# Four graph layers on one core: other distances, within 128 bytes, between the weights and what they are multiplied with

## What is computed

```
layer 0: q, k, v = x@Wq.T+bq, x@Wk.T+bk, x@Wv.T+bv     # 8 heads of 32
         P = softmax(where(adj == 0, -16384, q@k.T));  z = v
         4 times: z = 0.9 * P@z + 0.1 * v;              x = LN(x + z)
layer 1: P = softmax(where(adj == 0, -inf, (x@Wq)@(x@Wk).T / 16))   # one head
         x = LN(x + P@(x@Wv)@Wo + bo)
layer 2: 8 heads, P = softmax(where(adj == 0, -inf, q@k.T / sqrt(32)))
         x = LN(x + (P@v)@Wo + bo)
layer 3: for labels d = 1..4: agg_d = (adj == d) @ x / count_d
         out = relu(concat(agg_d)@Wd.T + bd)
         r, z = sigmoid(out@Wri.T + x@Wrh.T + b), sigmoid(out@Wzi.T + x@Wzh.T + b)
         n = tanh(out@Wni.T + bni + r*(x@Wnh.T + bnh)); x = LN((1-z)*n + z*x)
```

## The kernel before

| tensors | before |
|---|---|
| w_hi, w_lo, ident, wT (masks) | 0 |
| layer 0's q, k, z, v, E, PT | 32 |
| layer 1's q, v, E, PT, xT1 | 96 |
| layer 2's q, k, v, E, PT, and zT2 in the place of q and k | 64 |
| xw (also oT), agg, xT3, gates rT, zT, nT | 64 |
| y0 to y3, xn0, xn1 | 32 |
| xT_hi0 to 3, xT_lo0 to 3 | 64 |

## Time and profile before

### The profile page before, as it was taken

The page is one execution under the profiler, slowest core; times in us unless marked ns, Lnnn a source line. Parts: engine busy times, 40 slices in busy tenths (PEclk is TensorE's granted clock), DMA queues, the critical chain, the costliest instruction groups (busy, mean ns, idle before and its releaser), DMA issues.

```text
span 1605.4 us, 44598 instructions
## 1 busy us (share of the span) xinstructions
PE 1547.1 (96%) x17360; PEld 1405.8 (88%) x17360; DVE 1282.8 (80%) x3164; ACT 1237.9 (77%) x4074; POOL 697.0 (43%) x710
## 2 busy tenths in 40 slices
PE   7888999999999999999999999999999999999986
PEld 6777999899899989998998999899899999998875
DVE  3676888888888888888888888888888888888764
ACT  4677887787888788888878788887878888787652
POOL 1344444434454444445444444544444444444411
PEclk7999999999999999999999999999999999999999
DMA  5100000111110011011001101100110110000000
GB/s 201 34 25 28 28 28 15 34 35 29 34 35 28 15 35 34 28 35 35 27 15 35 35 28 35 34 28 15 35 35 28 35 35 27 15 28 25 18 8 13
DMA packets 71425, 51.64 MB, mean 32 GB/s; under 512 B 4400, under 2 KB 69936, under 8 KB 70576
## 3 DMA queue, kind: packets, MB, share of 16 engines
q1 hardware_dynamic: 71216, 48.79, 10.0%
HBM read 40.39 MB, written 8.39 MB: 30 GB/s over the span
## 4 chain that ended last, share of the span: by engine, by line
PE 67%; ACT 28%; DVE 2%; issue 1%; DMA 1%; POOL 0%; SPq 0%; POOLq 0%; DVEq 0%; ACTq 0%
ACT E L706 9%; PE bank_A L400 7%; ACT E L770 7%; PE bank_B L400 7%; PE bank_B L629 6%; PE bank_A L444 6%; PE bank_C L400 5%; PE bank_B L444 4%; PE bank_A L629 3%; PE bank_A L418 3%; PE bank_B L412 3%; ACT PT L712 2%; PE bank_A L430 2%; PE bank_X L550 2%; PE bank_A L528 2%; PE bank_B L438 2%
## 5 line engine op out<-in xcount | busy, mean ns | idle before, releaser
L850 POOL TENSOR_TENSOR E<-E,rsum 128x512 f32<-128x512 f32 x256 | 270.7, 1058 | 472.5 <-DVE rsum L1041 317.6
L858 POOL TENSOR_TENSOR rstd<-var,minus_half 128x2 f32<-128x2 f32 x128 | 93.7, 741 | 407.9 <-DVE var L995 407.9
L712 ACT ACTIVATE PT<-bank_C 128x512 f32<-128x512 f32 x128 | 85.8, 670 | 59.9 <-PE bank_C L438 59.9
L1002 DVE TENSOR_SCALAR y<-y,mv,rstd 128x256 f32<-128x256 f32 x192 | 93.0, 527 | 25.8 <-POOL rstd L858 25.8
L943 DVE COPY_PREDICATED_SCALAR bank_A<-absent,fill 128x512 f32 x128 | 92.3, 742 | 15.2 <-PE bank_B L430 14.4
L400 PE MATMUL bank_A<-xT_hi,w_hi 128*128 128x256 f32 x384 | 99.7, 284 | 0.0
L400 PE MATMUL bank_A<-xT_hi,w_lo 128*128 128x256 f32 x384 | 97.1, 277 | 0.0
L943 DVE COPY_PREDICATED_SCALAR bank_B<-absent,fill 128x512 f32 x128 | 94.7, 740 | 0.0
L770 ACT ACTIVATE E<-bank_A,nmax 128x128 f32<-128x128 f32 x256 | 92.4, 402 | 2.5 <-DVE nmax L1037 2.5
L706 ACT ACTIVATE E<-bank_B,nmax 128x128 f32<-128x128 f32 x256 | 94.2, 435 | 0.0
L706 ACT ACTIVATE E<-bank_A,nmax 128x128 f32<-128x128 f32 x256 | 90.8, 382 | 4.1 <-DVE nmax L946 4.1
(11 more groups left out here) (225 smaller groups left out, 6299.3 us busy)
## 6 DMA issues: line engine op xcount, KB each, us to landing
xt_in<-in_xt SPq DMA_DIRECT2D x64, 128.0 KB, 2.3
absent<-in_adj SPq DMA_DIRECT2D x64, 128.0 KB, 2.7
x_in<-in_x SPq DMA_DIRECT2D x32, 256.0 KB, 3.0
out<-y SPq DMA_DIRECT2D x32, 256.0 KB, 2.2
adj<-in_adj SPq DMA_DIRECT2D x32, 128.0 KB, 3.3
adjT<-in_adjt SPq DMA_DIRECT2D x32, 128.0 KB, 3.1
stage<-in_weights SPq DMA_DIRECT2D x3, 1024.0 KB, 11.3
row<-in_rows SPq DMA_DIRECT2D x1, 1024.0 KB, 7.9
```

The lines of the kernel that those rows point to most:

```text
L712: nc.scalar.activation(PT0[:, part].rearrange("p g c n -> p (g c n)"), C0[:, :], ACT.Copy, scale=1.0 - ALPHA).then_inc(pt0_ready.sem, 1)
L850: nc.gpsimd.tensor_tensor(e, e, rs[:, part].unsqueeze(2).to_broadcast([P, SB, P]), ALU.mult).then_inc(e_sig.sem, 1)
L858: nc.gpsimd.tensor_tensor(rstd[part][:], var[part][:], minus_half[:], ALU.pow)\
L1002: a = nc.vector.tensor_scalar(y[part][:, g, :], src[g], mv[part][:, g, 0:1], rstd[part][:, g:g + 1], ALU.subtract, ALU.mult)
```

## The change

One gap grows, one goes, and four small ones come in between the split inputs, which are now placed layer by layer (hi and lo of a layer side by side) and not all hi and then all lo. No instruction, wait, transfer, size or order differs on any engine; only addresses do.

```
-        sb("gap_1", [P, 16])
+        sb("gap_1", [P, 24])
         xw = sb("xw", [P, 8 * D])
         agg = sb("agg", [P, G, D])
...
         xn = [sb(f"xn{L}", [P, G, D]) for L in range(2)]
-        sb("gap_2", [P, 40])
-        xT_hi = [sb(f"xT_hi{L}", [P, NC, GN], F32R) for L in range(4)]
-        xT_lo = [sb(f"xT_lo{L}", [P, NC, GN], F32R) for L in range(4)]
+        xT_hi, xT_lo = [], []
+        for L, gap in enumerate((24, 16, 24, 8)):
+            sb(f"gap_x{L}", [P, gap])
+            xT_hi.append(sb(f"xT_hi{L}", [P, NC, GN], F32R))
+            xT_lo.append(sb(f"xT_lo{L}", [P, NC, GN], F32R))
         stats = [sb(f"stats{L}", [P, G, 6]) for L in range(4)]
```

## The result

The changed kernel takes 1622.2 us (median of 4 runs, 1620.83 to 1625.17), the kernel before beside it 1608.57 us (4 runs, 1606.68 to 1610.14): a ratio of 1.0087, 95% interval 1.0069 to 1.0104. It is slower, by 13.6 us. The forecast was 1602.7 us and the range 1594 to 1614: wrong in sign, and the time lies outside the range. It lies within 1 us of the slower of the two bounds that the prediction had worked out (1621.3) and then left out of its range.

What follows compares the result with a forecast made beforehand. TensorE was taken as the bound, by how densely its matmuls follow each other. From the profiled 1605.4 us, 5.2 off and 0.5 back gave 1600.7 of span; runs stand 2 above, so 1602.7 us, range 1594 to 1614.

Steps and rivals of the forecast that it cites:

- the two bounds: All moved tensors' matmuls wholly fast or wholly slow: 13.9 us won or lost, 1593.5 to 1621.3 us, without a third cadence.
- Part 4: Normalised y, agg, gates and layer 3's xT move along: transposes keep 109 ns, nothing lost on any engine.
- Part 5: The wait before layer 1's scores, for ScalarE, grows as TensorE gets faster: 0.5 us off the gain.
- Part 1: Layers 0 and 1, aggregation and labels, mostly slow, get cadences redrawn: half of 326 ns a round won, 5.2 us.
- Part 2: Layer 3's projections, moved to 96, taken as unchanged; an even draw would cost 72 ns a round, 2.3 us.
- Part 3: Layer 2 stays at 64 within 128 bytes and mostly fast, its output projection too; cost nothing.
- Rival A: Places don't matter, arrival alone may decide the cadence: 1607.4 us, give or take 3.4; chance 0.33.
- Rival B: Layer 3's projections and the labels fall wholly into the slow cadence: 1613.1 us, or 1617.1 without gains elsewhere; chance 0.21.
- Rival C: Moved 256-column matmuls take a third cadence: 109 ns, some 30 us won, 1577 us, or one slower than 118; chance 0.04.

Runs made afterwards that it cites:

- p_l3: Kernel before, hi and lo of a layer side by side, only layer 3's inputs moved, to 96 bytes beyond the weights within 256: 1614.59 us, 1.0029.
- a_l2: Changed kernel with layer 2's inputs 128 bytes further, back at distance 192; layers 0, 1 and 3 as changed: 1617.73 us, 1.0073 to the kernel before.
- e_move128: Kernel before with all xT_hi and xT_lo 128 bytes further, order of hi and lo kept: 1617.46 us, 1.0056.
- m_map: Small kernel, TensorE alone: chains of 36 matmuls over 16 pairs of operand places within 128 bytes, three kinds of start; two pairs reached 113.3 ns.
- m_dist: Small kernel, TensorE alone: chains of 24 matmuls at distances 0 to 992 bytes, behind transposes or plain products; steps 113.3 to 120.0 ns.
- m_start: Small kernel, TensorE alone: chains at distance 64 or 192 after 25 kinds of start; 117.5 ns at 64, mostly 113.3 at 192.
- e_l3: Kernel before with hi and lo of each layer side by side, xT 64 from the weights, but layer 3's inputs 32 bytes further: 1619.03 us, 1.0062.
- e_places: Changed kernel with its places, but all hi ahead of all lo as before: 1620.09 us, 1.0066 to the kernel before.
- e_pairs: Kernel before with hi and lo of each layer side by side, places within 128 bytes unchanged, xT from 192 to 64 within 256: 1616.52 us, 1.0046.
- p_l0: Kernel before, hi and lo of a layer side by side, only layer 0's inputs moved, to 160 bytes beyond the weights: 1611.17 us, 1.001.
- e_xw: Kernel before with hi and lo side by side, xT's distances kept, xw (with oT, agg, layer 3's xT, gates) 32 bytes further: 1608.58 us, 0.9998.

## Why the prediction was wrong, point by point

- **The bound** was read rightly. TensorE is the bound, nothing else moved, and 0.407 us a round of looser steps is the result. Part 4 holds: transposes of y (bank_X) and agg have records of 271 and 273 ns after, 272 and 273 before, and ScalarE's and VectorE's busy time is within 0.3% of what it was. Part 5 had a faster engine wait 0.5 us more; the slower one waits 142 ns a round less, 4.5 us in all. That a change of TensorE's pace is in part taken up by its waits was right; the wait was another, hidden behind overlapping records.
- **The premise that failed** stands in the second paragraph: "All float32r operands lie 64 bytes within 128 from the weights now. Yet there are two cadences". The unit is 256 bytes, and with it the projections stood at 192 and v0, v2, vo1, wo2, labels and aggregation at 64. The prediction drew from it "At the same clock and addresses both cadences occur". That sentence is true even by the right unit: q0 and q2, nh to ni in consecutive rounds, and the two label chains that it compares have the same distance each time (192, 192, 64). The step that failed is the next one, to carry this over to places where no matmul stood yet: at 32, 96, 160 and 224 no chain of 256-column matmuls of any whole kernel reached 113.3, so there was nothing to draw. The earlier trace rows could not warn of it, since it has the two distances alone and both have both cadences: at 192 means of 277 (oT, hi x hi) and 279 (k0 and q0, g1), at 64 of 276 (v2) to 280 (vo1, the aggregation). "A run then stays in its cadence" is true only once it is in it: before, k2 takes 118, 124 and 119 ns for the first three steps from 818.65 and then goes on at 113, and does much the same in every round, which makes its 115.2.
- **Part 1** (layers 0 and 1, aggregation and labels redrawn between both cadences, 5.2 us won) had no draw in it: its chains went to 32, 96, 160 and 224, where the whole kernels have no fast cadence and the small ones 116.7 to 120.0 ns. Measured: 107 + 11 + 18 + 1 = 137 ns a round more, inside the 181 that it allowed to be lost, where it took 163 won.
- **Part 2** (layer 3's projections unchanged) was the largest miss: 279 ns a round for 72 matmuls, more than its bound of 252, since nh and rh went to 119.7, past the 118 that it took for the slowest. p_l3 alone costs 4.7 us.
- **Part 3** (layer 2 stays and costs nothing) was wrong in fact. Within 256 it moved from 192 to 64, k2 and q2 went from 115.2 and 113.3 to 117.9 and 117.7, and wo2, which didn't move, from 113.7 to 117.7: 134 ns a round that the prediction put at nothing. a_l2, with layer 2's inputs back at 192, gets 4.5 us back. The check that the prediction named for itself, layer 2 at 276, would have shown it: bank_A's and bank_B's xT_lo are at 281.
- **The bounds**: 1621.3 at the slow end for a measured 1622.2, but not by its terms; that they meet within 1 us is in part luck. Against the 433 ns a round of that bound stand 137 for layers 0 and 1, aggregation and labels (it had 181), 279 for layer 3's projections (252), 134 for layer 2 (none) and 142 given back by waits (0.5 us in all, the other way): 408. What failed here was to leave this end out of the range because the cadence seemed a matter of luck at every distance, with the gain as likely as the loss.
- **Rival A** (places don't matter) falls with e_move128. With it falls the reading that the prediction gave to the Trainium skill's "SBUF — State Buffer", "SBUF: two separate sides" and "A bandwidth-pool intuition that's wrong", that addresses can't have an effect. What the page says is that TensorE waits on no one and that the weight load has a read port of its own; the small kernels leave TensorE all but alone, so they don't speak against the first. But TensorE's step still goes by where its own two operands lie, 113.3 against 120.0 ns. No run here shows what in the chip does it.
- **Rival B** (layer 3's long runs go slow) named the right place and sign, at 1613.1 or 1617.1, but for one layer of three and with a gain elsewhere that didn't come.
- **Rival C** (a third cadence) exists on the slow side, 118.5 to 120.0. The Trainium skill's "TensorE: Matmul & The Clock Gate", section "Wait — 56ns, not 53.3ns?", puts the step at N/2.4 GHz plus about 2.5 ns, for 256 columns an estimate of 109.2 ns; these float32r matmuls reached it at no distance.

## What to carry to other kernels

Where TensorE is the bound, read its step from start to start chain by chain, and set it against the distance between the operand loaded and the operand streamed, in the direction streamed minus loaded and within 256 bytes, not within the 128 that looks natural. Before a place is changed, write that table for every chain, those with exchanged roles and those that "stay" included, and ask which of its distances already have chains in the trace; for a distance that has none, a small kernel of chains gives the step. What a chain does also hangs on what runs ahead of it, so parts don't add up, and moving one operand can cost its neighbours' chains more than its own.

## What the runs showed of the hardware that was not expected

- float32r matmuls of 128x128 by 256 columns at the full clock step at 113.3, at 116.7 to 119.1 or at 120.0 ns by the distance within 256 bytes, taken in steps of 32 (m_map, m_dist); in these kernels 192 alone has 113.3. Moving everything by 32 bytes (e_shift) or the inputs by 256 (e_move256) changes nothing, moving the inputs by 128 costs 8 us.
- At 192 there are two stable cadences, 113.3 and 117.8, and small things choose: one bf16 matmul of 2 columns behind four transposes makes the following 36 matmuls slow (m_start).
- In the whole kernels 113.3 occurs at 192 and at 64, and at no other distance. At 64 it mostly follows a fast chain (v2, wo2 before), but g1 has it behind labels at 160 (e_l3) and wo2 behind a k0 of 119 ns at 160 (e_places, a_l2).
- What decides between the two cadences stays open. Behind labels at 160, k2 at 192 is slow in p_l3 (117.8) and fast in a_l2 (113.6). In e_pairs ri and ni recover at 192 behind a slow rh (113.9, 113.3), in e_move128, with the same distances and only the tensors' order different, they don't (117.3, 117.5).
- Label matmuls of 512 columns took 229.0 to 234.3 ns and were fastest at 64 behind certain chains (p_l0, e_xw), not at 192 (233.4).
- What in the memory or the load path makes 192 special was not tried, and no run here can tell.
